# Counting edges between blocks of nodes: cells of four nodes made as two halves of two nodes

## The chip, the cores and the metric

One core of one Trainium2 chip. The metric is the device time of one execution in microseconds (us). Engines in the profile: PE (TensorE matmul) and PEld (its weight loads), DVE (VectorE), ACT (ScalarE), POOL (GpSimd), SP (the queue that issues most transfers).

## The reference

A graph of 12500 nodes with 128 features and 212500 edges (200000 random ones and a loop for each node, sorted by target):

```python
h = jnp.maximum(_layernorm(x), 0.0)
m = jnp.where((edge_types == 0)[:, None], h[src] @ W_data.T + b_data, h[src] @ W_control.T + b_control)
x = x + relu(segment_sum(m, dst) + h @ W_self.T + b_self)
h = jnp.maximum(_layernorm(x), 0.0)
deg = segment_sum(ones, col)
norm = where(deg > 0, rsqrt(deg), 0)[row] * where(deg > 0, rsqrt(deg), 0)[col]
out = y = h
for _ in range(2):
    y = segment_sum(y[row] * norm[:, None], col)
    out = out + y
x = x + out / 3
```

## The kernel before

The work has a preparation, a first pass over the edges (k = 0) and two hops (k = 1, 2). The preparation normalises the nodes, makes a message row for each node and edge type in `typed_table`, and turns the edge lists so that one column holds 128 consecutive edges, a chunk. A test on DVE (`worst`, `checks`, `uneven`) chooses between a general branch and the branch described here, which these inputs take.

**First pass.** 1661 chunks stand in 208 groups of eight. For each chunk POOL issues one indirect gather (`gather`, L913) of 128 rows; for each group DVE makes one-hots of the targets (`make_hot`), PE multiplies them with the rows (`sum_group`, L1131), and DVE adds the sums into a window of nodes (`add_group`). A ring of four groups lies between POOL and PE: POOL waits for `summed` of four groups before. Loop slot i of every engine's program handles group i. Whenever 512 nodes (a batch) are complete, they are `cut` and finished: norm, next table `hop_table`, stores.

**Cells.** In the hops, the first 64 blocks of 128 target nodes (16 batches) aren't gathered edge by edge but multiplied with a count matrix `strips`, which says how many edges lead from each node to each node. It is made during the first pass, in slots 24 to 205, cell by cell. A cell is four target nodes and the 128 edges from the first edge of the first of them on. For each batch PE counts how many edges lie ahead of each cell (`place_cells`, with the triangle `before_cell`), DVE turns this into an offset (`cell_first`), and POOL fetches for 128 cells at once 128 pairs of numbers each, 1 KB, in one indirect gather (`gather_cells`, L953). PE transposes them (`turn_cells`), so that the edges of a cell lie on 128 lanes, and DVE stores two numbers for each edge: `cell_low` (the source within its block, made so that an edge of another cell matches nothing) and `cell_key` (source block and target within the cell).

Cells go in fours (a quad, 512 in all). `make_quad` on DVE makes two one-hots for a quad: `quad_low`, 4 x 128 columns (L1568), and `quad_hot`, 4 x 392 columns, 98 source blocks by 4 targets (L1571). `make_cells` on PE multiplies them for each cell, 392 columns (L1175), into one of three banks of `wide`, and follows each product by one warming product (`fill`, L1166, 512 columns whose result is not used); a slot has 16 fills in all, with or without quads. `keep_cell` on ACT copies each bank to bytes (L1043) and sets it free. DVE may be two quads ahead of PE. Each finished strip of 32 cells is stored by SP.

**Hops.** PE multiplies the count matrix with the table (`dense_step`, L1217), after ACT has cast the counts (L1055); POOL gathers the rows of the remaining edges. The first hop product needs all cells, and stands in PE's program behind the last group of the first pass.

Of the kernel before, what the change touches and what calls it, by code (L numbers as in the profile page):

```python
# [5 lines left out]
P = 128  # L6
# [6 lines left out]
NODE_BLOCKS = 4  # L13
# [11 lines left out]
CELL = 4  # L25
CELLS = P // CELL
QUAD = 4
QUADS = CELLS // QUAD
CELL_BANKS = 3
# [53 lines left out]
def gnn_kernel(nc, x, src, dst, edge_type, w_data, b_data, w_control, b_control, w_self, b_self, out):  # L83
# [171 lines left out]
    with ExitStack() as ctx:  # L255
# [51 lines left out]
        first_row, last_row = (region(pair_chunks) for _ in range(2))  # L307
        w_all, b_all = (region(KINDS * P) for _ in range(2))
# [17 lines left out]
        quad_hot = [region(QUAD * real_blocks * CELL // 2, BF16).rearrange("p (w n) -> p w n", w=QUAD) for _ in range(2)]  # L326
# [26 lines left out]
        before_cell = sbuf("before_cell", [NODE_BLOCKS, P], BF16)  # L353
# [14 lines left out]
        cell_first = sbuf("cell_first", [DENSE_BATCHES, 1], I32)  # L368
# [34 lines left out]
        dst_in = semaphore("dst_in")  # L403
        padded_x = semaphore("padded_x")
# [278 lines left out]
        def _(sp):  # L683
# [25 lines left out]
            for i in range(pairs):  # L709
# [8 lines left out]
                if i == EDGE_LOADS[2]:  # L718
                    edges(raw_dst, dst, dst_in)
                if i == EDGE_STEP + 4:  # L720
                    sp.wait_ge(base_made, 2)
                    sp.dma_start(base_dram.rearrange("a (k g) -> (a k) g", k=tiles), group_base[0:tiles, :]).then_inc(base_stored, 16)
                    sp.dma_start(ends_dram.rearrange("a (k g) -> k a g", k=tiles), chunk_ends[0:tiles]).then_inc(base_stored, 16)
# [141 lines left out]
        def _(pool):  # L865
# [13 lines left out]
            pool.memset(before_cell[:, :, :], 2.0).then_inc(lines_made, 1)  # L879
            pool.wait_ge(lines_made, 3)  # L880
            pool.affine_select(out=before_cell[:, :, :], in_=before_cell[:, :, :], compare_op=ALU.is_gt, fill=0.0,
                               base=0, pattern=[[-P, NODE_BLOCKS], [CELL, P]], channel_multiplier=-1).then_inc(lines_made, 1)
# [61 lines left out]
            with pool.Else():  # L944
# [3 lines left out]
                def gather_cells(s):  # L948
                    pool.wait_ge(pairs_stored, 16)
                    pool.wait_ge(cells_placed, s + 1)  # L950
                    if s >= 2:
                        pool.wait_ge(cells_turned, s - 1)
                    pool.indirect_dma_start(  # L953
                        out=cell_rows[s % 2].rearrange("p e n -> p (e n)"), out_offset=None, in_=runs,
                        in_offset=bass.IndirectOffsetOnAxis(ap=cell_first[:, s, :], axis=0)).then_inc(cells_in[s % 2], 16)
# [15 lines left out]
        def _(act):  # L971
# [65 lines left out]
            with act.Else():  # L1037
                def keep_cell(nth):
                    tile, w = divmod(nth, CELLS)
                    if w == 0 and tile >= 2:  # L1040
                        act.wait_ge(strips_stored[tile % 2], 16 * (tile // 2))
                    act.wait_ge(strip_made, nth + 1)
                    act.copy(count_strips[tile % 2][:, :, w * CELL:(w + 1) * CELL],  # L1043
                             wide[:, nth % CELL_BANKS, 0:real_blocks * CELL].rearrange("p (b n) -> p b n", n=CELL)
# [29 lines left out]
        def _(pe):  # L1074
# [79 lines left out]
            with pe.Else():  # L1154
# [14 lines left out]
                def make_cells(quad):  # L1169
                    pe.wait_ge(strip_hot_ready, quad + 1)  # L1170
                    for w in range(QUAD):
                        nth = quad * QUAD + w
                        if nth >= CELL_BANKS:
                            pe.wait_ge(strip_kept, nth - CELL_BANKS + 1)
                        pe.matmul(wide[:, nth % CELL_BANKS, 0:real_blocks * CELL], quad_low[quad % 2][:, w, :], quad_hot[quad % 2][:, w, :],  # L1175
                                  start=True, stop=True).then_inc(strip_made, 1)
                        fill(1)

                def place_cells(s, reads):

                    wait_small(reads)
                    pe.wait_ge(degree_read, s + 1)
                    for b in range(NODE_BLOCKS):
                        pe.matmul(small[:, 16:17], before_cell[:, b, :], batch_degree[:, b:b + 1], start=(b == 0), stop=(b == NODE_BLOCKS - 1))
                    for b in range(NODE_BLOCKS):
                        last = pe.matmul(small[:, 17:18], all_twos[:, :], batch_degree[:, b:b + 1], start=(b == 0), stop=(b == NODE_BLOCKS - 1))
                    last.then_inc(edges_counted, 1)

                def turn_cells(s, reads):
                    wait_small(reads)  # L1190
                    pe.wait_ge(cells_in[s % 2], 16 * (s // 2 + 1))
# [65 lines left out]
        def _(dve):  # L1257
# [8 lines left out]
            dve.tensor_scalar(cell_line[:, :], iota[:, 0:P], P, None, ALU.mult).then_inc(count_made, 1)  # L1266
# [85 lines left out]
            dve.tensor_copy(scratch[0], local[:, 0:pair_chunks]).then_inc(step, 1)  # L1352
            dve.wait_ge(base_in, 64)
            by_group = local[:, :].rearrange("p (g c) -> p g c", c=CHUNKS)
            dve.wait_ge(step, chain.done + 1)
            chain.done += 1
            done(dve.tensor_tensor(inside.rearrange("p (g c) -> p g c", c=CHUNKS), by_group,
                                   base_all[:, :].unsqueeze(2).to_broadcast([P, groups, CHUNKS]), ALU.subtract))
            dve.tensor_single_scalar(scratch[0], scratch[0], 2, ALU.logical_shift_right).then_inc(step, 1)
# [3 lines left out]
            done(dve.tensor_tensor(steps_up[:, 0:pair_chunks - 1], scratch[0][:, 1:pair_chunks], scratch[0][:, 0:pair_chunks - 1], ALU.subtract))  # L1363
            dve.tensor_reduce(worst[:, 1:2], steps_up[:, 0:pair_chunks - 1], AX_X, ALU.min)
# [24 lines left out]
            node_bits = (1 << 14) - CELL  # L1389
            dve.tensor_scalar(scratch[0], own_dst, node_bits, 5, ALU.bitwise_and, ALU.logical_shift_left)  # L1390
            done(dve.tensor_scalar(scratch[1], own_src, P - 1, None, ALU.bitwise_and))
            done(dve.tensor_tensor(pair_tile[:, :, 0], scratch[0], scratch[1], ALU.add))
            dve.tensor_scalar(scratch[0], own_src, 5, node_bits, ALU.logical_shift_right, ALU.bitwise_and)
            done(dve.tensor_scalar(scratch[1], own_dst, CELL - 1, None, ALU.bitwise_and))
# [116 lines left out]
            with dve.Else():  # L1511
# [48 lines left out]
                def make_quad(quad):  # L1560
# [9 lines left out]
                    columns = real_blocks * CELL  # L1570
# [4 lines left out]
                def take_places(s):  # L1575
# [3 lines left out]
                    dve.tensor_tensor(cell_first[:, s, :], small[:, 16:17], numbers_before[:, :], ALU.add).then_inc(cells_placed, 1)  # L1579
# [90 lines left out]
```

## Time and profile before

| | |
|---|---|
| median of 3 runs | 3896.39 us (3893.84 to 3898.22) |
| profiled execution | 3894.17 us |
| its span | 3892.4 us |
| mean granted TensorE clock | 0.944 of full speed |

The profiled execution's time is 1.8 us longer than the span that the trace covers. In the rows, "us" after the start is how long an instruction, or a merged run of them (x8), took; "mean ns" is one instruction's mean; "idle before" is idle time of the engine just before the group, with what ended it; "issue" means that the engine waited for nothing that the profile shows. A granted clock of 1.0 is 2.4 GHz and 0.5 is 1.2 GHz, so that a mean between them is a mix of both. One slot of the first pass issues eight row gathers.

### The profile page before, as it was taken

To read this page: it belongs to the slowest core of one execution; us is meant where nothing else is said; L and a number is where in the kernel's file an instruction comes from. 1 tells how busy PE (TensorE), PEld (TensorE's weight loads), DVE (VectorE), ACT (ScalarE), POOL (GpSimd) and SP (SyncE) were. 2 spreads that over 40 slices of the span, in tenths; PEclk is the share of its full clock that TensorE was granted. 3 is DMA by queue.
4 is the path that set the end of the run, shared out by engine and by line. 5 is a ranking of instruction groups with operands and counts; after the bars stand their busy time and mean duration, and the time that the engine had idled before them with its cause. 6 is when DMAs were issued, how large, how long until landed. Compare 5 with 4: busy or idle time off the path is not lost.

```text
span 3892.4 us, 48593 instructions
## 1 busy us (share of the span) xinstructions
PE 3314.4 (85%) x16748; PEld 2354.8 (60%) x16748; DVE 2290.2 (59%) x3557; ACT 2417.2 (62%) x3174; POOL 2742.7 (70%) x2915
## 2 busy tenths in 40 slices
PE   6576777877787777777877799999999799999999
PEld 4344444444444444444444478787887688888887
DVE  7523888988898898888989823233233222222223
ACT  4100454544455454444545499888988699999997
POOL 2677777777777777777777747776777277777775
PEclk9888999998999999999989999999999899999999
DMA  6322334334334343344333478888888988888886
GB/s 194 90 64 64 114 114 130 114 121 133 114 116 128 114 130 114 114 131 124 125 118 115 130 220 258 250 257 245 263 262 243 283 259 251 249 254 248 245 247 203
DMA packets 505886, 675.98 MB, mean 174 GB/s; under 512 B 74854, under 2 KB 430065, under 8 KB 497443
## 3 DMA queue, kind: packets, MB, share of 16 engines
q1 hardware_dynamic: 395075, 408.99, 33.6%
q0 software_dynamic: 109696, 263.44, 22.9%
q8 instruction: 135, 2.21, 0.2%
q14 instruction: 116, 0.95, 0.1%
q10 hardware_dynamic: 864, 0.39, 0.0%
HBM read 510.59 MB, written 162.00 MB: 173 GB/s over the span
## 4 chain that ended last, share of the span: by engine, by line
PE 40%; POOL 39%; issue 13%; DVE 3%; DMA 3%; ACT 2%; SPq 0%; DVEq 0%; POOLq 0%; ACTq 0%
POOL rows L913 38%; PE wide L1217 34%; PE sums_bank L1131 4%; ACT strip_ring L1055 2%; DMA stage<-strips 1%; PE wide L1094 1%; DMA hop_table<-scaled 1%; DVE stage L1571 0%; DMA rows<-typed_table,index 0%; PE turned_bank L1166 0%; DVE big L1270 0%; DVE rows L1310 0%; POOL stage L953 0%; PE turned_bank L1231 0%; PE wide L1175 0%
## 5 line engine op out<-in xcount | busy, mean ns | idle before, releaser
L913 POOL DMA_INDIRECT rows<-typed_table,index x1661 | 1589.2, 957 | 505.9 <-issue 504.5
L1055 ACT CAST strip_ring<-stage 128x2048 fp32r<-128x2048 uint8 (+1 forms) x800 | 1438.9, 1869 | 139.5 <-PE wide L1217 116.8
L1217 PE MATMUL wide<-strip_ring,table_parts 128*128 128x512 f32 x6272 | 1467.7, 393 | 42.8 <-ACT strip_ring L1055 42.7
L913 POOL DMA_INDIRECT hop_rows<-hop_table,index x1162 | 1113.9, 959 | 521.7 <-issue 333.7
L1043 ACT CAST stage<-wide 128x392 uint8<-128x392 f32 x2048 | 849.1, 500 | 925.1 <-PE wide L1175 923.1
L1217 PEld LDWEIGHTS wide<-strip_ring,table_parts 128*128 128x128 f32 x6272 | 1176.2, 189 | 287.3 <-ACT strip_ring L1055 31.3
L1166 PE MATMUL turned_bank<-all_twos 128*128 128x512 bf16 x3328 | 1142.1, 397 | 0.0
L1175 PE MATMUL wide<-stage 128*128 128x392 bf16 x2048 | 703.7, 344 | 275.8 <-DVE stage L1571 274.7
L1571 DVE TENSOR_TENSOR stage<-count_up,stage 128x1568 bf16<-128x1568 f32 x512 | 910.4, 1778 | 0.0
L1546 DVE SCALAR_TENSOR_TENSOR sums<-sums_bank,in_upper,sums 128x128 f32 (+1 forms) x500 | 174.1, 348 | 951.6 <-PE sums_bank L1131 922.5
L1131 PE MATMUL sums_bank<-rows,hot 128*128 128x129 f32 x3322 | 468.9, 300 | 207.2 <-DMA rows<-typed_table,index 191.9
L1131 PEld LDWEIGHTS sums_bank<-rows,hot 128*128 128x128 f32 x3322 | 446.7, 213 | 253.1 <-issue 213.8
L1166 PEld LDWEIGHTS turned_bank<-all_twos 128*128 128x128 bf16 x3328 | 340.2, 102 | 344.3 <-issue 62.1
L1175 PEld LDWEIGHTS wide<-stage 128*128 128x128 bf16 x2048 | 206.9, 101 | 549.0 <-DVE stage L1571 401.5
L1568 DVE TENSOR_TENSOR stage<-count_up,stage 128x512 bf16<-128x512 f32 x512 | 348.1, 680 | 131.6 <-PE wide L1175 131.0
L1520 DVE TENSOR_TENSOR hot<-count_up,local 128x1024 f32<-128x1024 f32 x208 | 252.0, 1212 | 0.1
L1464 DVE TENSOR_TENSOR scaled<-scaled,index 128x512 fp32r<-128x512 f32 (+1 forms) x25 | 17.1, 682 | 304.7 <-ACT index L1023 304.7
L1520 DVE TENSOR_TENSOR hop_hot<-count_up,local 128x1024 fp32r<-128x1024 f32 x146 | 177.1, 1213 | 0.0
L1546 DVE SCALAR_TENSOR_TENSOR sums<-sums_bank,base_all,sums 128x128 f32 (+1 forms) x500 | 170.8, 342 | 0.5
L1131 PEld LDWEIGHTS sums_bank<-hop_rows,hop_hot 128*128 128x128 f32 x1162 | 159.1, 191 | 11.9
L1131 PE MATMUL sums_bank<-hop_rows,hop_hot 128*128 128x256 f32 x1162 | 162.3, 283 | 0.0
L1015 ACT ACTIVATE batch_spread<-batch_spread 128x8 f32<-128x8 f32 x25 | 5.3, 210 | 251.2 <-DVE batch_spread L1281 251.2
(146 smaller groups left out, 839.4 us busy)
## 6 DMA issues: line engine op xcount, KB each, us to landing
stage<-strips SPq DMA_DIRECT2D x384, 512.0 KB, 4.4
strips<-stage SPq DMA_DIRECT2D x64, 1568.0 KB
rows<-typed_table,index POOLq DMA_INDIRECT x1661
hop_rows<-hop_table,index POOLq DMA_INDIRECT x1162, 3.8
resid<-xin SPq DMA_DIRECT2D x50, 256.0 KB, 4.0
xin<-resid SPq DMA_DIRECT2D x50, 256.0 KB
typed_table<-rows SPq DMA_DIRECT2D x49, 256.0 KB, 2.1
table_parts<-hop_table SPq DMA_DIRECT2D x14, 896.0 KB, 9.8
```

The source lines that it names most:

```text
L913: pool.indirect_dma_start(out=into, out_offset=None, in_=tables[k], in_offset=bass.IndirectOffsetOnAxis(ap=index[:, chunk:chunk + 1], axis ...
L1043: act.copy(count_strips[tile % 2][:, :, w * CELL:(w + 1) * CELL], wide[:, nth % CELL_BANKS, 0:real_blocks * CELL].rearrange("p (b n) -> p ...
L1055: act.copy(strip_ring[:, number % STRIP_RING].rearrange("p t b n -> p t (b n)")[:, :, 0:columns], counts_ring[n % COUNT_RING][:, :, ahead: ...
L1094: last = pe.matmul(wide[:, i % 2 * PAIR + b, 0:KINDS * P], normed_t[i % 2][:, b * P:(b + 1) * P], w_all[:, :], start=True, stop=True)
L1131: last = pe.matmul(sums_bank[:, bank, 0:columns], hots[:, place, c, :], values[:, slot, c, 0:columns], start=(c == 0), stop=(c == size - 1))
L1166: pe.matmul(turned[:, 0:4 * P].rearrange("p (n f) -> p n f", n=4), all_twos[:, :], all_twos[:, :].unsqueeze(1).to_broadcast([P, 4, P]), st ...
L1175: pe.matmul(wide[:, nth % CELL_BANKS, 0:real_blocks * CELL], quad_low[quad % 2][:, w, :], quad_hot[quad % 2][:, w, :], start=True, stop=Tr ...
L1217: last = pe.matmul(wide[:, nth % 4, 0:BATCH].rearrange("p (t n) -> p t n", t=NODE_BLOCKS), table_parts[:, b, part, :], strip_ring[:, numbe ...
L1520: dve.tensor_tensor((hot if o < groups else hop_hot)[:, place, :, :], counting(CHUNKS, P), local[:, group * CHUNKS:(group + 1) * CHUNKS].u ...
L1546: last = dve.scalar_tensor_tensor(out=into, in0=sums_bank[:, o % 2, part * P:part * P + columns], scalar=inside_tile, in1=into, op0=ALU.mu ...
L1568: dve.tensor_tensor(quad_low[place], counting(QUAD, P), cell_low[:, cells].unsqueeze(2).to_broadcast([P, QUAD, P]), ALU.is_equal)
L1571: dve.tensor_tensor(quad_hot[place], counting(QUAD, columns), cell_key[:, cells].unsqueeze(2).to_broadcast([P, QUAD, columns]), ALU.is_equ ...
```

## The change

A cell of four nodes is fetched and multiplied as two halves of two nodes. Each half has 64 lanes: its edges are the 64 from the first edge of its first node on. So `quad_hot` has 98 x 2 columns for each cell and not 98 x 4; lanes 0 to 63 serve the first two nodes, lanes 64 to 127 the last two. Each cell's product becomes two, each over 64 lanes of the array and 196 columns; the halves go to different banks, and two cells share a bank, so that a bank again holds 392 columns. The fills follow behind a quad's products instead of between them. ACT copies as many banks, in runs of two bytes instead of four. For every batch there are two triangles, two offsets and two gathers of 64 pairs (512 bytes) for each cell. The test now asks that the edge 64 places on belongs to another pair of nodes, for which the targets are loaded a second time, shifted by 64 edges (`raw_ahead`).

```diff
-        quad_hot = [region(QUAD * real_blocks * CELL // 2, BF16).rearrange("p (w n) -> p w n", w=QUAD) for _ in range(2)]
+        quad_hot = [region(QUAD * real_blocks * HALF // 2, BF16).rearrange("p (w n) -> p w n", w=QUAD) for _ in range(2)]
...
                 if i == EDGE_LOADS[2]:
                     edges(raw_dst, dst, dst_in)
+                    sp.dma_start(raw_ahead.rearrange("p (k e) -> p k e", k=PAIR_TILES),
+                                 dst[HALF_EDGES:HALF_EDGES + pair_chunks * P].rearrange("(k p e) -> p k e", p=P, e=P)).then_inc(dst_ahead_in, 16)
...
-            pool.memset(before_cell[:, :, :], 2.0).then_inc(lines_made, 1)
+            for half in before_cell:
+                pool.memset(half[:, :, :], 2.0).then_inc(lines_made, 1)
...
+            for h, half in enumerate(before_cell):
+                pool.affine_select(out=half[:, :, :], in_=half[:, :, :], compare_op=ALU.is_gt, fill=0.0,
+                                   base=h * HALF, pattern=[[-P, NODE_BLOCKS], [CELL, P]], channel_multiplier=-1).then_inc(lines_made, 1)
...
-                    pool.indirect_dma_start(
-                        out=cell_rows[s % 2].rearrange("p e n -> p (e n)"), out_offset=None, in_=runs,
-                        in_offset=bass.IndirectOffsetOnAxis(ap=cell_first[:, s, :], axis=0)).then_inc(cells_in[s % 2], 16)
+                    for h in range(P // HALF_EDGES):
+                        pool.indirect_dma_start(
+                            out=cell_rows[s % 2][:, h * HALF_EDGES:(h + 1) * HALF_EDGES, :].rearrange("p e n -> p (e n)"), out_offset=None, in_=runs,
+                            in_offset=bass.IndirectOffsetOnAxis(ap=cell_first[:, s, h:h + 1], axis=0)).then_inc(cells_in[s % 2], 16)
...
-                    act.copy(count_strips[tile % 2][:, :, w * CELL:(w + 1) * CELL],
-                             wide[:, nth % CELL_BANKS, 0:real_blocks * CELL].rearrange("p (b n) -> p b n", n=CELL)
+                    pair, h = divmod(w, 2)
+                    nodes = count_strips[tile % 2][:, :, pair * 2 * CELL:(pair + 1) * 2 * CELL].rearrange("p b (w n) -> p w b n", n=CELL)
+                    act.copy(nodes[:, :, :, h * HALF:(h + 1) * HALF],
+                             wide[:, nth % CELL_BANKS, 0:2 * real_blocks * HALF].rearrange("p (w b n) -> p w b n", w=2, n=HALF)
...
-                    for w in range(QUAD):
-                        nth = quad * QUAD + w
-                        if nth >= CELL_BANKS:
-                            pe.wait_ge(strip_kept, nth - CELL_BANKS + 1)
-                        pe.matmul(wide[:, nth % CELL_BANKS, 0:real_blocks * CELL], quad_low[quad % 2][:, w, :], quad_hot[quad % 2][:, w, :],
-                                  start=True, stop=True).then_inc(strip_made, 1)
-                        fill(1)
+                    columns = real_blocks * HALF
+                    for pair in range(QUAD // 2):
+                        for w in range(2):
+                            for h in range(2):
+                                nth = quad * QUAD + pair * 2 + h
+                                if w == 0 and nth >= CELL_BANKS:
+                                    pe.wait_ge(strip_kept, nth - CELL_BANKS + 1)
+                                edges = slice(h * HALF_EDGES, (h + 1) * HALF_EDGES)
+                                last = pe.matmul(wide[:, nth % CELL_BANKS, w * columns:(w + 1) * columns], quad_low[quad % 2][edges, pair * 2 + w, :],
+                                                 quad_hot[quad % 2][edges, pair * 2 + w, :], start=True, stop=True)
+                                if w:
+                                    last.then_inc(strip_made, 1)
+                    fill(QUAD)
...
-            dve.tensor_copy(scratch[0], local[:, 0:pair_chunks]).then_inc(step, 1)
+            dve.tensor_single_scalar(scratch[0], raw_dst[:, 0:pair_chunks], 1, ALU.logical_shift_right).then_inc(step, 1)
...
-            dve.tensor_single_scalar(scratch[0], scratch[0], 2, ALU.logical_shift_right).then_inc(step, 1)
+            dve.tensor_single_scalar(scratch[1], raw_ahead, 1, ALU.logical_shift_right).then_inc(step, 1)
...
-                    columns = real_blocks * CELL
+                    columns = real_blocks * HALF
```

In `place_cells` the counting products become twelve for a batch where there were eight (four more with one column each); `take_places` makes two offsets in one instruction, and the offsets, keys and shifts elsewhere follow from 64 lanes and two nodes.

## Rows read from the trace of the kernel before

**Rows 1.** Page, busy times: busy us, share of the span, instructions.

```profile
PE 3314.4 (85%) x16748; PEld 2354.8 (60%) x16748; DVE 2290.2 (59%) x3557; ACT 2417.2 (62%) x3174; POOL 2742.7 (70%) x2915
```

**Rows 2.** Three stretches: start to end, us busy (instructions) by engine, granted clock, DMA.

```profile
150.00:200.00 50.00, 36.97 (x191) 23.37 (x189) 9.11 (x17) 0.00 (x0) 37.81 (x41) 0.88 0.22 59
1500.00:2000.00 500.00, 393.07 (x2155) 229.89 (x2155) 440.05 (x572) 243.55 (x590) 378.75 (x399) 0.94 0.38 119
2500.00:3000.00 500.00, 490.47 (x2333) 411.99 (x2332) 157.21 (x310) 448.00 (x261) 358.35 (x371) 0.99 0.84 255
```

**Rows 3.** Waits of POOL over the span: us, times, longest.

```profile
POOL rows L913 <- issue: 504.5, 1656, 0.3
...
POOL rows L913 <- PE sums_bank L1131: 1.2, 4, 0.3
```

**Rows 4.** Timeline of POOL, its last gather of the first pass.

```profile
2232.75 0.97 POOL L913 DMA_INDIRECT rows<-typed_table,index  x1 [0.30 <-issue]
```

**Rows 5.** Timeline of PE, from the last chunk sum to the first hop product.

```profile
2238.07 1.70 PE L1131 MATMUL sums_bank<-rows,hot 128*128 128x129 f32 x10 [2.68 <-DMA rows<-typed_table,index]
2239.57 4.99 PE L1166 MATMUL turned_bank<-all_twos 128*128 128x512 bf16 x16
2244.21 14.88 PE L1217 MATMUL wide<-strip_ring,table_parts 128*128 128x512 f32 x64
```

**Rows 6.** Groups by line and shape: busy us, mean ns, idle before.

```profile
L913 POOL DMA_INDIRECT rows<-typed_table,index x1661 | 1589.2, 957 | 505.9 <-issue 504.5 <-PE sums_bank L1131 1.2
...
L1571 DVE TENSOR_TENSOR stage<-count_up,stage 128x1568 bf16<-128x1568 f32 x512 | 910.4, 1778 | 0.0
L1043 ACT CAST stage<-wide 128x392 uint8<-128x392 f32 x2048 | 849.1, 500 | 925.1 <-PE wide L1175 923.1
...
L1568 DVE TENSOR_TENSOR stage<-count_up,stage 128x512 bf16<-128x512 f32 x512 | 348.1, 680 | 131.6 <-PE wide L1175 131.0
...
L1023 ACT CAST index<-scaled 128x512 fp32r<-128x512 f32 x24 | 14.7, 614 | 44.2 <-DMA hop_table<-scaled 44.2
...
L953 POOL DMA_INDIRECT stage<-edge_pairs,cell_first x16 | 15.1, 946 | 4.9 <-issue 4.9
...
L998 ACT COPY rows<-turned_bank 128x256 f32<-128x256 f32 x25 | 9.2, 369 | 11.9 <-PE turned_bank L1086 11.7
...
L1184 PE MATMUL wide<-batch_degree,before_cell 128*128 128x1 bf16 x64 | 3.9, 164 | 0.0
```

**Rows 7.** Line L913 from 400 to 2200 us: ns min/median/max.

```profile
L913 POOL DMA_INDIRECT rows<-typed_table,index x1416: 940/945/1586, 399.3 to 2199.0; - x177
```

**Rows 8.** Timeline of PE in one slot: start us, us.

```profile
1503.93 1.95 PE L1131 MATMUL sums_bank<-rows,hot 128*128 128x129 f32 x16
1505.71 1.03 PE L1166 MATMUL turned_bank<-all_twos 128*128 128x512 bf16 x4
...
1508.15 0.33 PE L1175 MATMUL wide<-stage 128*128 128x392 bf16 x1
1508.32 0.38 PE L1166 MATMUL turned_bank<-all_twos 128*128 128x512 bf16 x1
1508.53 0.33 PE L1175 MATMUL wide<-stage 128*128 128x392 bf16 x1
```

**Rows 9.** Waits of all engines, the row of the cells' products.

```profile
PEld wide L1175 <- DVE stage L1571: 401.5, 287, 9.3
```

**Rows 10.** Timeline of POOL in the preparation.

```profile
2.98 0.64 POOL L881 TENSOR_SCALAR_AFFINE_SELECT before_cell<-before_cell 128x512 bf16<-128x512 bf16 x1
...
34.63 1.57 POOL L895 CAST big<-big 128x1664 f32<-128x1664 int32 x1 [26.09 <-DMA big<-in_src]
...
48.10 1.57 POOL L899 CAST big<-big 128x1664 f32<-128x1664 int32 x1 [6.79 <-DMA big<-in_dst]
...
118.52 0.15 POOL L919 MEMSET rows<- 128x32 f32 x1 [56.83 <-DMA typed_table<-rows]
118.82 1.54 POOL L913 DMA_INDIRECT rows<-typed_table,index  x1
```

## What the change will do to the time

> **What bounds the kernel now.** I read the busy shares first, then a table by stretches, then the waits of POOL, then the chain's turn from the first stage to the hops, and last the groups of instructions. The busy shares [rows 1] name no bound: POOL 70%, DVE 59%, both averages over two stages. The stretches [rows 2] separate them. From 1500 to 2000 us, in the first pass over the edges, DVE is busy 440 of 500 us and looks like the limit; POOL is busy only 379. In the hops DVE falls to 157 of 500 and PE is busy 490 of 500: there PE sets the pace. What paces the first pass is seen in POOL's waits [rows 3]: over all its gathers it waited 1.2 us for another engine, and 504.5 us for nothing that the profile shows, 1656 times 0.305 us, the gap between two gathers in a row. POOL never stops; its 76% "busy" is a full queue. The stretch from 150 to 200 us proves that DVE does not slow it: DVE is busy 9 of 50 us there, before the first cells, and POOL is busy 37.8 of 50 us; from 1500 to 2000 us, with DVE at 88%, POOL is busy 37.9 of 50 [rows 2]. From the first gather at 118.8 us to the end of the last at 2233.7 [rows 4, 10] there are 1661 row gathers and 16 cell gathers: 2114.9 / 1677 = 1.261 us each. So the first pass lasts as long as POOL has gathers to issue, and the hops as long as PE has products.
>
> PE enters the hops 10.5 us after POOL's last gather ends: its last chunk sum stands behind that gather's landing, 16 warming products follow, and the first hop product starts at 2244.2 us [rows 4, 5]. That tail hangs on POOL's last gather, so a later gather moves all that follows.
>
> **Part by part.**
>
> POOL's cell gathers. Each batch's one gather becomes two of half the length: 16 more instructions. The old one takes 946 ns and 4.9 / 16 = 0.306 us of gap [rows 6]. Its rows are 1 KB long; the row gather L913 moves 512 B rows, as the halves will, and has a median of 945 ns [rows 7]. Cost goes by instruction, not by bytes. 16 x (0.946 + 0.306) = 20.0 us, on the path, since POOL has no idle time to take it. Lower end: 16 x 0.946 = 15.1 us, if the second of a pair had no gap of its own; upper end: the longest gather between 400 and 2200 us, 1.586 us [rows 7], each time: 16 x 1.892 = 30.3 us. I take 20.0: 1656 gaps agree.
>
> DVE's one-hots. The wide one falls from 1568 to 784 columns. From the two forms in [rows 6], (1778 - 680) / (1568 - 512) = 1.04 ns a column, so 784 columns cost 680 + 272 x 1.04 = 963 ns: 815 ns saved 512 times, 417 us of DVE time. On the path this is worth nothing: POOL waited 1.2 us for what DVE feeds. It only takes from PE the 401.5 us that its products waited for DVE [rows 9].
>
> PE's products. Four products of 392 columns become eight of 196 over 64 lanes each, and the four warming products ("fills") that stood between them now stand behind them. By the slot timeline [rows 8] a slot (one group of eight chunks) costs PE 1.78 us of sums, 16 fills of 0.21 and 11.25 products of 0.17, 7.1 us, while POOL gives it 8 gathers, 10.1 us. No row shows a product over half the lanes. Lower end: the two halves of a pair of banks run side by side, 0.08 us for two. Upper end: each runs alone, from start to end like the 392-column product, 0.33 us of which 0.17 is columns, so 0.16 more for each half: 8 x (0.083 + 0.16) = 1.94 us a quad, with four fills 2.8 us. Between them I take: products in line, and a new wait. With three banks the fourth product's bank comes free only when ACT has copied the first, 0.41 us (three products of 0.083, one way through the array of 0.164) and 0.50 us [rows 6] after the quad began; three more products, 0.25, four fills, 0.84: 2.0 us. What changes between whole and half arrays I price by the one-column product, 0.164 us from start to end [rows 6], twice a quad: 2.3 us. A slot is then 1.78 + 4.75 x 0.21 + 2.81 x 2.3 = 9.3 us (512 quads in 182 slots are 2.81), and 9.7 if the 7.1 us of columns run at the mean clock granted from 1500 to 2000 us, 0.94 [rows 2]. POOL will give it 10.1 + 20.0 / 182 = 10.2 us. It stays covered, cost 0, but the cover shrinks from 3 us to 0.5.
>
> A rule of the Trainium skill speaks against the change here: "TensorEngine Tiling (Array Packing)", Key Properties, says that a change of tiling mode drains TensorE. This kernel would change it twice a quad, 1024 times; by the one-column row above that is 168 us of PE time, all of it hidden if PE keeps its cover, and none of it in the sum. No run here shows the drain yet.
>
> ACT's copies. Still 2048 of 392 elements, now written in runs of 2 bytes and not 4. The old 500 ns lies on the line through two copies with long runs, 369 ns for 256 and 614 for 512 elements [rows 6]: (614 - 369) / 256 x 136 + 369 = 499. Runs of four cost nothing, so I take nothing for runs of two. Even doubled, 2 x 849 us fits into the 1860 us of the slots with cells.
>
> The rest. POOL's second triangle (a memset and a select, 0.64 us for the select) ends in a wait of 26.1 us for the source list [rows 10]. The extra load of the shifted targets on SP's queue (1152 columns) stands in front of message stores; POOL waited 6.8 us for the load before it, of 1664 columns [rows 10], so at most 6.8 us lie behind it, but the stores follow DVE's pace until 118.5 us and POOL waits 56.8 us for the last of them: 0. DVE's check swaps a cast for a shift of the same size: 0; POOL has 32 gathers (40 us) to issue before it asks for the result. Four more one-column products a batch on PE: 0, under the same cover. The new test wants no two neighbouring nodes with over 64 edges together; in the reference's inputs the most is 62, so the branch stays.
>
> The tail. Less DVE work could shorten what follows the last gather; the last sum waits for the landing, not for DVE [rows 5], so 0, with a lower bound of -10.5 us if the whole tail went.
>
> **Sum.** Span 3892.4 + 20.0 = 3912.4 us; the profiled execution took 3894.17 us, 1.8 more than its span, so 3914.2. The median of the runs, 3896.39, lies 2.2 us above the profiled execution: 3916.4 us, 0.5% slower. The likeliest case's own range: +15.1 - 10.5 to +30.3, 3901 to 3927.
>
> **Rivals.** (A) PE becomes the bound of the first pass. For it: the new bank wait, the change of arrays, the lost cover; against: PE waits 401.5 us for DVE today. It decides from (10.2 - 2.8) / 2.81 = 2.63 us a quad. At the upper end, 2.8 us, a slot takes 10.65 us against 10.07 today: 0.58 x 182 = 106 us, 4002 us. (B) Not slower: POOL's long gathers shrink. L913 lasts 1589.2 us where 1661 at the median would last 1569.6 [rows 6, 7]: 19.6 us are lost to gathers of up to 1.586 us. If DVE's wide one-hots caused these, halving them would give back up to 19.6 us: 3896.8 us. It decides from 12.2 us given back, where the loss falls under 7.8 us. Against it: POOL's busy share is the same with and without the one-hots [rows 2]. (C) Faster: B in full and the tail's 10.5 us too: 3886 us.
>
> **How the numbers follow.** POOL's 16 gathers and nothing else: 0.74. A: 0.15, spread from 3916 to 4002. B: 0.08. C: 0.03. The range 3905 to 3950 leaves out the upper half of A, most of B, and C, and the lowest tail of the first case: 0.2. A measurement of this kernel can tell about 0.2%, 7.8 us. Slower: the first case without its low end, 0.72, and A, 0.15: 0.87. Same: 0.10. Faster: 0.03.
>
> **What would show it.** Right: 32 cell gathers of about 0.946 us in the profile after, POOL's waits for PE still near nothing, its last gather of the first pass at about 2252.8 us, PE's first hop product some 10 us later, hops of the same length; DVE's wide one-hot near 963 ns and DVE's busy share in 1500 to 2000 us near 72%. Wrong: POOL rows waiting for PE's sums in the slots with cells (A), a mean of L913 near 945 ns (B), or a first hop product less than 10 us after the last gather.

## The result

The changed kernel takes 4754.18 us (median of 4 runs, 4752.69 to 4754.63) where the kernel before takes 3896.18 us on the same chip: a ratio of 1.2202, interval 1.2181 to 1.2223. That is 858 us more. The forecast of 3916.4 us and its range up to 3950 us are far off; the direction alone is right. The first hop product starts at 3101.39 us and did at 2244.21 [rows 5], so 857 us of the loss lie in the first pass; from there to the end it is 1649.5 us here and 1648.2 before.

The busy shares on the page of the changed kernel answer to [rows 1]:

```profile
PE 3893.6 (82%) x18860; PEld 2549.3 (54%) x18860; DVE 1909.9 (40%) x3558; ACT 3403.1 (72%) x3174; POOL 2764.4 (58%) x2933
```

POOL has 18 instructions more and 22 us more busy time, DVE 380 us less. Two engines went up by far more: PE by 579 us, though its products have as many columns as before, and ACT by 986 us, though it executes as many instructions as before. The stretch from 1500 to 2000 us, beside the second row of [rows 2]:

```profile
1500.00:2000.00 500.00, 376.75 (x1878) 193.19 (x1877) 233.16 (x402) 349.38 (x404) 264.88 (x278) 0.72 0.26 82
```

POOL executes 278 instructions in these 500 us, before 399: eight of them take 14.4 us in place of 10.0. The clock granted to PE is 0.72, a mix with more than half of the time at 1.2 GHz, and was 0.94. No engine is full. So the waits are read next (line, what it waits for, us in total, times, longest):

```profile
POOL rows L922 <- PE sums_bank L1143: 847.5, 172, 12.2
ACT stage L1055 <- PE wide L1191: 819.2, 270, 45.2
PEld wide L1191 <- ACT stage L1055: 804.5, 1044, 1.4
```

The first row had 1.2 us in [rows 3]. POOL now waits for PE's sums, and PE's sums stand behind the cells' products, which wait 1044 times for ACT to empty a bank; ACT in turn waits as long for PE. Two engines that wait for each other pace the first pass. The groups by form say which of their instructions grew, beside [rows 6]:

```profile
L1055 ACT CAST stage<-wide 128x392 uint8<-128x392 f32 x2048 | 1838.6, 1121 | 821.8 <-PE wide L1191 819.2
L922 POOL DMA_INDIRECT rows<-typed_table,index x1661 | 1592.6, 959 | 1301.0 <-PE sums_bank L1143 847.5 <-issue 453.5
...
L1191 PE MATMUL wide<-stage 64*128 64x196 bf16 x4096 | 582.0, 293 | 675.2 <-ACT stage L1055 566.9 <-DVE stage L1592 106.2
L1592 DVE TENSOR_TENSOR stage<-count_up,stage 128x784 bf16<-128x784 f32 x512 | 493.3, 963 | 0.0
...
L963 POOL DMA_INDIRECT stage<-edge_pairs,cell_first x32 | 30.2, 944 | 9.8 <-issue 9.8
```

The one-hot at 963 ns and the 32 cell gathers at 944 ns are as forecast. ACT's copy is not: the same 392 elements from fp32 to bytes took 849.1 us in all and take 1838.6. How that looks around one slot (timelines of PE, then of ACT, and last one of ACT in the kernel before):

```profile
1503.41 1.04 PE L1178 MATMUL turned_bank<-all_twos 128*128 128x512 bf16 x4
1504.38 0.26 PE L1191 MATMUL wide<-stage 64*128 64x196 bf16 x1
1504.89 0.34 PE L1191 MATMUL wide<-stage 64*128 64x196 bf16 x3 [0.25 <-ACT stage L1055]
1505.76 0.25 PE L1191 MATMUL wide<-stage 64*128 64x196 bf16 x1 [0.53 <-ACT stage L1055]
1506.63 0.51 PE L1191 MATMUL wide<-stage 64*128 64x196 bf16 x3 [0.62 <-ACT stage L1055]
1507.07 1.89 PE L1178 MATMUL turned_bank<-all_twos 128*128 128x512 bf16 x4
1508.89 0.72 PE L1191 MATMUL wide<-stage 64*128 64x196 bf16 x5
1510.52 0.50 PE L1191 MATMUL wide<-stage 64*128 64x196 bf16 x3 [0.91 <-ACT stage L1055]
1510.95 1.89 PE L1178 MATMUL turned_bank<-all_twos 128*128 128x512 bf16 x4
1512.64 0.64 PE L1212 MATMUL wide<-identity,stage 128*128 128x128 f32 x2
1513.06 3.54 PE L1143 MATMUL sums_bank<-rows,hot 128*128 128x129 f32 x16
```

```profile
1502.05 7.16 ACT L1055 CAST stage<-wide 128x392 uint8<-128x392 f32 x8 [3.55 <-PE wide L1191]
1509.43 3.67 ACT L1055 CAST stage<-wide 128x392 uint8<-128x392 f32 x4 [0.22 <-PE wide L1191]
```

```profile
1510.05 1.65 ACT L1043 CAST stage<-wide 128x392 uint8<-128x392 f32 x4 [0.64 <-PE wide L1175]
```

Eight copies take 7.16 us, 0.895 us each in a row, where four took 1.65 us in a row before. And PE's own work becomes slow in the course of the slot. The four fills at 1503.41 still take 1.04 us. Then the eight half products of a quad come in ones and threes, with 0.25, 0.53 and 0.62 us of waiting for ACT between them. The four fills behind them take 1.89 us and the group's sixteen sums 3.54 us, in place of 1.03 and 1.95 [rows 8]. So 2.4 and 1.2 GHz stand side by side in one slot.

### The profile page after: what moved, and what is told of

Its sections match the earlier page's. It is cut to its first block, busy times and chain, and to the rows that moved or that the text cites. A ratio compares the mean times of both kernels' runs of the same rounds, so it can differ in the third digit from the quotient of the medians.

```text
span 4750.9 us, 52837 instructions
## 1 busy us (share of the span) xinstructions
PE 3893.6 (82%) x18860; PEld 2549.3 (54%) x18860; DVE 1909.9 (40%) x3558; ACT 3403.1 (72%) x3174; POOL 2764.4 (58%) x2933
## 4 chain that ended last, share of the span: by engine, by line
PE 63%; ACT 25%; POOL 4%; DVE 4%; issue 2%; DMA 1%; SPq 0%; DVEq 0%; ACTq 0%; POOLq 0%
PE wide L1236 29%; ACT stage L1055 23%; PE turned_bank L1178 14%; PE sums_bank L1143 12%; PE wide L1191 5%; POOL rows L922 4%; ACT strip_ring L1067 1%; PE wide L1106 1%; ACT scaled L994 1%; DMA hop_table<-scaled 1%; DMA stage<-strips 0%; DVE hot L1541 0%; DVE stage L1592 0%; DVE xin L1479 0%; DVE big L1291 0%
## 5 line engine op out<-in xcount | busy, mean ns | idle before, releaser
L1055 ACT CAST stage<-wide 128x392 uint8<-128x392 f32 x2048 | 1838.6, 1121 | 821.8 <-PE wide L1191 819.2
L922 POOL DMA_INDIRECT rows<-typed_table,index x1661 | 1592.6, 959 | 1301.0 <-PE sums_bank L1143 847.5
L1191 PE MATMUL wide<-stage 64*128 64x196 bf16 x4096 | 582.0, 293 | 675.2 <-ACT stage L1055 566.9
L1178 PE MATMUL turned_bank<-all_twos 128*128 128x512 bf16 x3328 | 1127.2, 480 | 0.0
L1191 PEld LDWEIGHTS wide<-stage 64*128 64x128 bf16 x4096 | 189.5, 99 | 1185.9 <-ACT stage L1055 804.5
L1143 PEld LDWEIGHTS sums_bank<-rows,hot 128*128 128x128 f32 x3322 | 638.4, 286 | 151.6 <-issue 122.8
L1143 PE MATMUL sums_bank<-rows,hot 128*128 128x129 f32 x3322 | 629.7, 368 | 85.7 <-DMA rows<-typed_table,index 71.5
L1592 DVE TENSOR_TENSOR stage<-count_up,stage 128x784 bf16<-128x784 f32 x512 | 493.3, 963 | 0.0
```

Of the source, the lines that this page charges most:

```text
L922: pool.indirect_dma_start(out=into, out_offset=None, in_=tables[k], in_offset=bass.IndirectOffsetOnAxis(ap=index[:, chunk:chunk + 1], axis ...
L1055: act.copy(nodes[:, :, :, h * HALF:(h + 1) * HALF], wide[:, nth % CELL_BANKS, 0:2 * real_blocks * HALF].rearrange("p (w b n) -> p w b n", ...
L1143: last = pe.matmul(sums_bank[:, bank, 0:columns], hots[:, place, c, :], values[:, slot, c, 0:columns], start=(c == 0), stop=(c == size - 1))
L1178: pe.matmul(turned[:, 0:4 * P].rearrange("p (n f) -> p n f", n=4), all_twos[:, :], all_twos[:, :].unsqueeze(1).to_broadcast([P, 4, P]), st ...
L1191: last = pe.matmul(wide[:, nth % CELL_BANKS, w * columns:(w + 1) * columns], quad_low[quad % 2][edges, pair * 2 + w, :], quad_hot[quad % 2 ...
L1592: dve.tensor_tensor(quad_hot[place], counting(QUAD, columns), cell_key[:, cells].unsqueeze(2).to_broadcast([P, QUAD, columns]), ALU.is_equ ...
```

## The experiments

First theory: ACT's copies, because they write runs of two bytes, set the pace. Rivals: the copy is slow because its access has one loop more; the half products and their bank waits (A of the prediction); the cut gathers. When the copies turned out to explain 351 of the 858 us, theories on PE's clock and on the order of PE's program followed. The expectations state each one as it stood.

**The changed kernel with long runs.** ACT writes the bank's 392 bytes in one run; the counts lie in other places of the strip. All else is the changed kernel.

```diff
-act.copy(nodes[:, :, :, h * HALF:(h + 1) * HALF],
-         wide[...].rearrange("p (w b n) -> p w b n", w=2, n=HALF))
+act.copy(count_strips[tile % 2].rearrange("p b n -> p (b n)")[:, w * real_blocks * CELL:(w + 1) * real_blocks * CELL],
+         wide[:, nth % CELL_BANKS, 0:2 * real_blocks * HALF])
```

> The changed kernel, but ACT writes each bank's 392 counts as one run of 392 bytes; the counts then lie in other places than the hops read them from, so the result is not the reference's. Theory 1 (ACT's copy got slower because it writes runs of 2 bytes, 0.90 us a copy where it took 0.41, and PE waits for it): the mean copy falls from 1121 ns back to about 500, a slot falls from 15.1 us to POOL's 10.2, and the time to 3916 to 3960 us. Theory 2 (PE's half products, the change of array mode and the fills that no longer stand between the products): copies fall to 500 ns all the same, but PE stays slow and the time stays over 4500 us.

3912.99 us beside 3891.78, ratio 1.0054 (1.0038 to 1.0070). With this one access undone, 837 of the 858 us are gone (858.0 less 21.2). Its groups:

```profile
L1055 ACT CAST stage<-wide 128x392 uint8<-128x392 f32 x2048 | 879.5, 489 | 939.7 <-PE wide L1191 932.6 <-issue 4.0
...
L1191 PE MATMUL wide<-stage 64*128 64x196 bf16 x4096 | 416.0, 262 | 363.8 <-ACT stage L1055 251.1 <-DVE stage L1592 112.7
```

The copy takes 489 ns again. The half products still wait for ACT, 251.1 us over 512 quads, 0.49 us each, and POOL waits 1.8 us for PE: that new wait is real and hidden. So all but 21 us of the loss hang on the short runs, by whatever path.

**The kernel before with short runs.** The other side: nothing of the change but the order in which ACT writes the same bytes to the same places.

```diff
-act.copy(count_strips[tile % 2][:, :, w * CELL:(w + 1) * CELL],
-         wide[...].rearrange("p (b n) -> p b n", n=CELL))
+act.copy(count_strips[tile % 2][:, :, w * CELL:(w + 1) * CELL].rearrange("p b (u n) -> p u b n", u=2),
+         wide[...].rearrange("p (b u n) -> p u b n", u=2, n=2))
```

> The kernel before with one change: ACT writes the same counts in runs of 2 bytes (a loop over two halves of the four nodes outside the loop over blocks). Nothing else moves. Theory 1: the copy takes 0.9 us and more where it took 0.41 (mean 500 ns), 2048 x 0.49 = 1000 us more of ACT, and the time rises to 4300 to 4750 us. Theory 2: the time stays within 3900 to 3960 us, as ACT has the room.

4242.55 us beside 3891.78, ratio 1.0900 (1.0875 to 1.0926), 351 us more; the first theory had expected 4300 at least. The copies cost what they cost in the changed kernel, but the whole costs well under half of it:

```profile
L1043 ACT CAST stage<-wide 128x392 uint8<-128x392 f32 x2048 | 1826.3, 1133 | 330.6 <-PE wide L1175 330.6
```

```profile
1500.00:2000.00 500.00, 360.15 (x1810) 164.69 (x1811) 375.33 (x495) 424.39 (x495) 318.74 (x336) 0.96 0.31 100
```

The difference is read in two places: the granted clock is 0.96 in this stretch, not 0.72, and ACT waits 330.6 us for PE, not 819.2.

**The kernel before with as many loops and runs of four bytes.**

```diff
+act.copy(count_strips[...].rearrange("p (u b) n -> p b u n", u=2),
+         wide[...].rearrange("p (u b n) -> p b u n", u=2, n=CELL))
```

> The kernel before with the copy's blocks walked in another order (two halves of the blocks in the inner loop), so that the copy has the same count of loops as the changed kernel's, but still writes runs of 4 bytes. Theory 1 (length of the run): 500 ns a copy and 3896 us. Rival within it, Theory 3 (the third loop of the access pattern costs, not the run): about 1.1 us a copy and the time of the kernel before with short runs.

3892.04 us beside 3891.78, ratio 1.0002 (0.9992 to 1.0013); the copy 849.2 us, 500 ns. The third loop is free; the length of the run is what costs.

**The kernel before with runs of one byte.**

```diff
+act.copy(count_strips[...].rearrange("p b n -> p n b"),
+         wide[...].rearrange("p (b n) -> p n b", n=CELL))
```

> The kernel before, copies in runs of 1 byte (one loop over the four nodes outside the blocks), same counts in the same places. If a copy's time goes by runs (98 runs: 0.41 us, 196 runs: 0.87 us): 392 runs, 1.75 us a copy, and 5500 to 6000 us. If any run under 4 bytes costs the same for each element: 0.87 us a copy and 4240 us, as with 2 bytes.

5929.95 us in one run. Its copy, in the groups by form:

```profile
L1043 ACT CAST stage<-wide 128x392 uint8<-128x392 f32 x2048 | 3600.0, 2227 | 243.0 <-PE wide L1175 241.5
```

Busy time over count, copies overlapping at their ends taken once: 0.415 us for 98 runs of four bytes, 0.892 us for 196 of two, 1.758 us for 392 of one. From two bytes to one it is 0.866 / 196 = 4.4 ns a run, and 196 runs at 4.5 ns are the 0.88 us of two bytes. At four bytes, 0.415 / 98 = 4.2 ns a run; but one run of 392 bytes takes no less, 879.5 / 2048 = 0.429, so that there the elements set the time and no longer the runs. In this kernel and in the one with two-byte runs ACT also reads the bank in shorter pieces, of one and of two elements. For two bytes that costs nothing: the changed kernel reads its bank in order and pays the same (1838.6 us beside 1826.3). For one byte the two sides were not tried apart.

The stretch of this kernel, with a clock of 0.65:

```profile
1500.00:2000.00 500.00, 295.74 (x1037) 131.22 (x1037) 216.29 (x283) 465.60 (x280) 177.80 (x186) 0.65 0.18 57
```

**The kernel before with two gathers for each batch.** Its cells' gather is cut into two of 64 pairs; DVE makes the second offset, one small instruction more a batch.

```diff
-pool.indirect_dma_start(out=cell_rows[s % 2]..., in_offset=...(ap=cell_first[:, s, :], axis=0))
+for h in range(2):
+    pool.indirect_dma_start(out=cell_rows[s % 2][:, h * 64:(h + 1) * 64, :]..., in_offset=...(ap=cell_first[:, s, h:h + 1], axis=0))
...
+dve.scalar_tensor_tensor(out=cell_first[:, s, 1:2], in0=small[:, 16:17], scalar=128.0, ...)
```

> The kernel before with each cell gather cut into two of half the length: the term that the prediction put at 20.0 us, alone. If POOL is the bound of the first pass and cost goes by instruction: 16 x 1.252 = 20.0 us more, 3916 us, 32 gathers of 946 ns. If it is hidden: 3896 us.

3910.11 us beside 3891.78, ratio 1.0049 (1.0031 to 1.0068), 18.3 us more. The gathers, 32 of 943 ns, with 9.8 us of gaps:

```profile
L954 POOL DMA_INDIRECT stage<-edge_pairs,cell_first x32 | 30.2, 943 | 9.8 <-issue 9.8
```

That is the forecast's one term by itself: 20.0 us lie inside the interval of 12 to 26 us.

**Short runs and the fills behind, whole products.** The second experiment, with the fills where the change puts them.

```diff
                         ...start=True, stop=True).then_inc(strip_made, 1)
-                        fill(1)
+                    fill(QUAD)
```

> The kernel before with short runs and, in addition, the four fills of a quad behind its four products. Theory 1b: 4600 to 4750 us, the granted clock in the first pass near 0.73 and not 0.96. Rival (half products and paired banks): 4240 us as with short runs alone.

4349.62 us beside 3894.46, ratio 1.1170 (1.1147 to 1.1192), 104 us more than the second experiment (each less its own kernel before). The expectation missed: if the place of the fills had taken the clock away, it would be near 0.73; it is 0.96.

```profile
1500.00:2000.00 500.00, 332.43 (x1731) 170.66 (x1729) 359.05 (x473) 404.85 (x472) 301.83 (x318) 0.96 0.31 98
```

**The changed kernel with its fills between the pairs.**

```diff
-                    fill(QUAD)
+                        fill(QUAD // 2)   # inside the loop over pairs
```

> The changed kernel with its four fills of a quad put back: two behind the first pair of cells, two behind the second, instead of four behind both. Copies stay in runs of 2 bytes. Theory 1b (the 490 us by which the changed kernel exceeds the kernel before with short runs and 20 us of gathers come from fills that no longer fill PE's wait for ACT): the time falls to 4260 to 4550 us. Rival (they come from the half products and from two banks being tied up together): 4700 us and more.

4572.52 us beside 3894.46, ratio 1.1742 (1.1718 to 1.1765): 180 us are given back (each less its own kernel before), and the clock hardly moves:

```profile
1500.00:2000.00 500.00, 415.09 (x2000) 193.25 (x1998) 249.38 (x440) 367.26 (x432) 284.80 (x297) 0.74 0.28 88
...
L1055 ACT CAST stage<-wide 128x392 uint8<-128x392 f32 x2048 | 1820.7, 1127 | 658.8 <-PE wide L1191 658.8
```

The time lies between what the theory and its rival expected. So the place of the fills is worth something in both kernels, and is not what holds the clock down in the changed one.

**The changed kernel bank by bank.** Maybe the order was to blame: the change begins a pair of banks together, so that PE needs two free banks of three. Here both halves of a bank are made before the next bank is asked for, with one fill behind each bank, as the kernel before does.

```diff
-                        for w in range(2):
-                            for h in range(2):
-                                if w == 0 and nth >= CELL_BANKS: ...wait
+                        for h in range(2):
+                            if nth >= CELL_BANKS: ...wait
+                            for w in range(2):
...
+                            fill(1)
```

> The changed kernel with PE's work in the order of the kernel before: the two half products of one bank, one fill, then the next bank; each bank waits for ACT by itself. Copies stay in runs of 2 bytes. Open is what holds the rest, 4754 less 4242 (before with short runs) less 20 (gathers) = 492 us. Theory 1c (two banks are begun together and PE's fills stand behind, so ACT runs dry while PE does sums and fills): 4260 to 4300 us, granted clock near 0.96. Theory 1d (half products leave PE at its lower clock, at which sums and fills take twice as long, whatever the order): 4450 us and more, granted clock in the first pass under 0.85.

4595.61 us beside 3895.94, ratio 1.1797 (1.1762 to 1.1831), with a clock of 0.76:

```profile
1500.00:2000.00 500.00, 447.41 (x1992) 217.87 (x1991) 243.43 (x417) 368.86 (x424) 278.11 (x292) 0.76 0.29 89
```

That theory falls. Only 158 us are given back, fewer than by moving the fills alone (180), so at this clock it costs nothing to fill the banks in pairs. In the order of the kernel before the half products still cost 349 us more than whole ones with the same runs, at a clock of 0.76.

**The changed kernel with twice the fills.** Four behind each pair, eight a quad: more work for PE, nothing taken away.

```diff
-                    fill(QUAD)
+                        fill(QUAD)   # inside the loop over pairs
```

> The changed kernel with four fills behind each pair of cells, eight a quad and not four: more work for PE, in the time in which it waits for ACT. Theory 1d, if the fills bring the clock to its upper level: a pair takes 0.33 + 4 x 0.21 = 1.2 us of PE beside 1.75 us of ACT's two copies, and the time is 4260 to 4400 us, less than with two fills behind each pair (4572). If the clock stays at its lower level: 0.8 + 4 x 0.43 = 2.5 us a pair, PE sets the pace, and the time is 5000 us and more. Theory 1c: 4572 us or a little more, as the order of products and banks is the same.

4386.41 us beside 3895.94, ratio 1.1260 (1.1227 to 1.1292): 188 us less than with half as many fills in the same places and 368 us less than the changed kernel (each less its own kernel before). The stretch, ACT's copies, and a group's sums on PE's timeline, back at their old 1.95 us:

```profile
1500.00:2000.00 500.00, 431.86 (x2585) 199.15 (x2583) 269.32 (x470) 398.50 (x463) 305.89 (x320) 0.96 0.31 94
...
L1055 ACT CAST stage<-wide 128x392 uint8<-128x392 f32 x2048 | 1832.0, 1129 | 465.2 <-PE wide L1191 465.1
```

```profile
1510.74 1.95 PE L1143 MATMUL sums_bank<-rows,hot 128*128 128x129 f32 x16
```

**The halves dealt out so that a bank holds four neighbouring nodes.** Can the change be kept and ACT's run of four bytes too? Here two cells in a row share eight nodes: their first halves hold nodes 0 and 1, and 2 and 3, their second halves 4 and 5, and 6 and 7. A bank, which takes one half of two cells, then holds four nodes in a row; PE writes its two products interleaved, and ACT's copy is that of the kernel before.

```diff
-base=h * HALF, pattern=[[-P, NODE_BLOCKS], [CELL, P]]
+base=h * CELL, pattern=[[-P, NODE_BLOCKS], [2 * CELL, P // 2], [HALF, 2]]
...
-pe.matmul(wide[:, nth % CELL_BANKS, w * columns:(w + 1) * columns], ...)
+pe.matmul(wide[:, nth % CELL_BANKS, 0:2 * columns].rearrange("p (b w n) -> p b w n", w=2, n=HALF)[:, :, w, :], ...)
...
-act.copy(nodes[:, :, :, h * HALF:(h + 1) * HALF], ...)
+act.copy(count_strips[tile % 2][:, :, w * CELL:(w + 1) * CELL], ...)
...
```

> The changed kernel with its halves dealt out otherwise: of eight neighbouring nodes, the first half lanes of two cells take nodes 0 to 3 and the second half lanes nodes 4 to 7, and PE writes the two cells interleaved into a bank, so that a bank holds four neighbouring nodes for each block and ACT's copy is again the one of the kernel before, in runs of 4 bytes. All else as in the changed kernel, and the result is the reference's. Theory 1: 3912 us, the kernel before with two gathers; copies 500 ns. If PE's interleaved writes cost something: more than 3930 us.

3915.99 us beside 3894.46, ratio 1.0059 (1.0043 to 1.0076). The change without its short runs costs 21.5 us, and the interval takes in the 18.3 of the cut gathers alone. Timelines of PE and of ACT in one slot, then the stretch:

```profile
1506.82 0.42 PE L1189 MATMUL wide<-stage 64*128 64x196 bf16 x5
1507.73 0.34 PE L1189 MATMUL wide<-stage 64*128 64x196 bf16 x3 [0.49 <-ACT stage L1053]
1508.01 1.04 PE L1176 MATMUL turned_bank<-all_twos 128*128 128x512 bf16 x4
1508.98 0.42 PE L1189 MATMUL wide<-stage 64*128 64x196 bf16 x5
```

```profile
1507.19 1.72 ACT L1053 CAST stage<-wide 128x392 uint8<-128x392 f32 x4 [5.14 <-PE wide L1189]
```

```profile
1500.00:2000.00 500.00, 400.80 (x2718) 214.18 (x2713) 329.28 (x566) 250.94 (x586) 378.71 (x399) 0.92 0.39 120
```

POOL executes 399 instructions in these 500 us, exactly as before, with DVE at 329 us in place of 440: the work that DVE is spared buys nothing. No version here beats the kernel before.

## Why the prediction was wrong

**The step that failed** is the one on ACT's copies: "Runs of four cost nothing, so I take nothing for runs of two. Even doubled, 2 x 849 us fits into the 1860 us of the slots with cells." Both halves are wrong. The duration: rows of copies with long runs and one with runs of four bytes lay on one line, and I read off that runs do not matter. They showed only that at four bytes the elements still set the time. At two bytes the copy's busy time goes from 0.415 to 0.892 us.

The cover: ACT's time looked free because it waited 923 us for PE [rows 6]. That wait is not room. A copy needs a product in a bank, there are three banks for a quad's four products, and while PE does a group's sums and fills ACT can't work ahead. The second experiment prices it: 2048 copies at 0.892 us are 1826 us, and 182 times, once a slot, ACT still waits for PE, 330.6 us in all. Together 2157 us do not fit into 1860. With ACT's other work the stretch from the first copy to the last grows from 1846 us (383.8 to 2230.0) to 2199 (380.9 to 2579.6), and the time by 351 us.

A second term failed with it: the sum let PE's columns run at the clock of the kernel before, 0.94. In the changed kernel it is 0.72, and PE does not stay covered.

**From 351 to 858 us.** In the kernels with slow copies ACT does little else in the first pass than copy and wait for PE. Each as a difference to the kernel before with two-byte runs, times less those of their own kernel before:

| kernel | copies, us | waits for PE, us | both less 2156.9 | time less that of two-byte runs |
|---|---|---|---|---|
| before, two-byte runs | 1826.3 | 330.6 | 0 | 0 |
| the same, fills behind | 1828.5 | 433.1 | 104.7 | 104.4 |
| before, one-byte runs (one run) | 3600.0 | 241.5 | 1684.6 | 1684.7 |
| changed, twice the fills | 1832.0 | 465.1 | 140.2 | 139.7 |
| changed, fills between | 1820.7 | 658.8 | 322.6 | 327.3 |
| changed, bank by bank | 1844.0 | 659.9 | 347.0 | 348.9 |
| changed | 1838.6 | 819.2 | 500.9 | 507.2 |

The last two columns agree within 7 us. That is bookkeeping, since copies and waits must fill ACT's time: it says where the time went, not why. What the changed kernel loses beyond its copies is time in which ACT waits for PE, and the 20 us of the gathers need not show in its time, as POOL waits 847.5 us in any case.

Why it waits longer is shown in part. Of the 507 us, 180 come back when two of a quad's four fills are moved between its pairs; the clock stays low (0.72 and 0.74), so they belong to the order of PE's work. Another 188 come back when the fills are doubled in those places, which adds work for PE. With that the clock goes from 0.74 to 0.96, the sums take 1.95 us again, and ACT's waits fall by 194 us (658.8 to 465.1): as added fills could only delay PE at an equal clock, this gain goes by the clock. 140 us remain over whole products with two-byte runs, also in ACT's waits. How much of them is the added fills themselves, how much that they stand in groups (moving the fills behind the quad costs 104 us by itself in the kernel before), and how much the banks filled in pairs was not tried apart and stays open.

What takes the clock down is neither the half products nor copies of 0.89 us alone: half products with fast copies have 0.92 (the dealt halves), whole products with two-byte runs 0.96, half products with two-byte runs 0.72 to 0.76 in three orders of PE's program. With whole products it falls too once the copies are slower still: 0.65 with one-byte runs. Why half products leave the clock lower than whole ones when both wait for the same copies, the runs do not tell; that four more fills a quad bring it back, they do.

**What held.** The cut gathers: 20.0 us forecast, 18.3 measured alone, and 21.5 for the change with runs of four bytes. With the dealt halves POOL's last row gather starts at 2247.20 us, not at 2252.8: the first one started 2.0 us earlier, and the row gathers took 1585.5 us in place of 1589.2. The first hop product follows at 2259.49, 15.3 us later than in [rows 5], and the hops end another 5 us later still, for a reason that stays open. So the 21.5 us come near the forecast partly by luck: POOL was done 5.6 us earlier than forecast, and what follows took some 6 us longer. The one-hot at 963 ns. DVE's time worth nothing. The wait for the third bank: forecast 0.91 us after the quad began, and the sixth half product of the dealt halves, the first to need a copied bank, starts at 1507.73, 0.91 us after 1506.82. A quad of 2.3 us, measured 2.16 (1506.82 to 1508.98), under the bound of 2.63. DVE's forecast share of 72% was a slip: 440 less 417 x 500 / 1860 is 328 of 500 us, and the dealt halves show 329.

**The rivals.** Rival A's picture, POOL waiting for PE's sums, is what came; its cause is not the half products' duration or the change of arrays, which the dealt halves have too at 21.5 us, and its 4002 us had no room for it. For the mode change: four fills in front of half products take 0.97 us from the first fill to the first product (1508.01 to 1508.98 with the dealt halves), in front of whole products 0.87 (1506.61 to 1507.48 with two-byte runs), so it costs 0.1 us going in. Going out it costs as much: among single instructions, the last half product before 1508.01 starts at 1507.83, and the fill follows 0.18 us later where its columns are 0.083. The 0.164 us that I had put on each change was too much. The Trainium skill, "TensorEngine Tiling (Array Packing)", Key Properties, says that changing the mode drains TensorE; the trace agrees, with about 0.1 us at each change. B and C are out: of the 19.6 us of long gathers DVE's relief gave back 3.7 with the dealt halves, far from the 12.2 from which B decides, and the tail did not shrink: 11.3 us from the last gather's end to the first hop product, where it had 10.5.

## What to carry to other kernels

An engine's wait is not free room when the engine that it waits for also waits for it. With few buffers between them only part of the wait can be filled (here 923 us of waiting took 977 us more of copies at a price of 351), so price a slower instruction over one turn, its busy time and the wait that stays, and not by the share of the span. When an edit changes the runs that an engine writes, take the price from a row with runs of that length, or call it unknown and give it an end of the range; a line through longer runs says nothing below them. And when TensorE begins to wait, look at the granted clock in the same stretch: all its other work may pay too, as the sums did here (1.95 to 3.54 us).

## What was not expected of the hardware

ACT's copy of 392 elements from fp32 in a bank to bytes costs by the run below four bytes, about 4.5 ns each: 0.415 us at four bytes, 0.892 at two, 1.758 at one, and no more for a third loop (849.2 us in all, beside 849.1). At one byte the reads were short as well.

Doing more can be faster: eight fills a quad in place of four, nothing removed, took the kernel from 4572.52 to 4386.41 us, and the clock from 0.74 to 0.96. Half products do run side by side: with the dealt halves they start in pairs, the two of a pair 0.003 us apart and the next pair 0.09 us later, and five start and end within 0.42 us.
